# Cross-attention on one core: gram in nine matmuls per group, packed diagonal blocks, TensorE's orders rewritten

## What is computed

```python
probs_t = jax.nn.softmax(scores_t, axis=-1)
text_out = jnp.einsum('bhst,bhtd->bhsd', probs_t, v_t)
...
qsem = _l2norm(jnp.einsum('bhst,bte->bhse', probs_t, text_ehs))
sem = jnp.einsum('bhse,bne->bhsn', qsem, _l2norm(ip_ehs))
fused = attn_scores + SEM_SCALE * sem
probs_ip = jax.nn.softmax(fused, axis=-1) * spatial_mask[None, None, :, None]
...
out = (text_out + ip_out) @ W_out + b_out + residual
```

## Time and profile before

| | us |
|---|---|
| median of 3 runs | 386.72 |
| lowest and highest | 385.99, 387.68 |
| span of the profiled execution | 384.5 |
| busy in it: PE | 374.8 |
| DVE | 225.0 |
| ACT | 213.2 |
| POOL | 208.1 |

### The profile page before, as it was taken

The page is one execution under the profiler, slowest core; times in us unless marked ns, Lnnn a source line. Parts: engine busy times, 40 slices in busy tenths (PEclk is TensorE's granted clock), DMA queues, the critical chain, the costliest instruction groups (busy, mean ns, idle before and its releaser), DMA issues.

```text
span 384.5 us, 9489 instructions
## 1 busy us (share of the span) xinstructions
PE 374.8 (97%) x3610; PEld 320.3 (83%) x3610; DVE 225.0 (59%) x498; ACT 213.2 (55%) x498; POOL 208.1 (54%) x229
## 2 busy tenths in 40 slices
PE   8999999998999999999999999999999999999996
PEld 6879898777888888888888888888888888888774
DVE  4998462774457536664556646664556656654454
ACT  6834145575556554646556554646555476458742
POOL 7020470675448652796248642796258443855972
PEclk9999999999999999999999999999999999999999
DMA  8999998276027420571227430581207310001000
GB/s 252 321 241 182 201 213 157 82 162 140 9 72 166 78 72 2 157 147 24 76 73 162 81 87 2 160 147 20 77 2 174 59 43 3 2 2 57 2 3 31
DMA packets 30001, 37.88 MB, mean 99 GB/s; under 512 B 14378, under 2 KB 27163, under 8 KB 29275
## 3 DMA queue, kind: packets, MB, share of 16 engines
...
## 4 chain that ended last, share of the span: by engine, by line
PE 84%; DMA 6%; DVE 5%; ACT 2%; issue 1%; SPq 1%; DVEq 0%; ACTq 0%
PE PR L1078 39%; PE Y L1078 27%; PE O L1078 9%; PE P L1078 7%; DMA qst<-ma 3%; DVE mx L950 2%; DMA Vt<-wk 2%; PE PR L1269 1%; DMA qd<-kst 1%; PE PR L1206 1%; DVE kst L904 0%; DVE kst L902 0%; ACT big L796 0%; SPq L507 0%; SPq L427 0%
## 5 line engine op out<-in xcount | busy, mean ns | idle before, releaser
L620 POOL TENSOR_TENSOR pb<-pb 128x448 f32<-128x448 f32 x78 | 89.1, 1143 | 97.2 <-DVE pb L974 91.8
L950 DVE TENSOR_REDUCE mx<-PR 112x1 f32<-112x371 f32 x160 | 82.0, 537 | 75.2 <-PE PR L1078 74.9
L1078 PE MATMUL Y<-er,Gh 128*128 128x448 f32 x240 | 95.2, 397 | 0.7 <-ACT er L800 0.3
L974 DVE TENSOR_TENSOR pb<-big,Y 128x448 f32<-128x448 f32 x120 | 72.7, 620 | 33.6 <-PE Y L1078 33.4
L1078 PE MATMUL Y<-er,Gl 128*128 128x448 f32 x240 | 87.2, 363 | 0.0
L796 ACT ACTIVATE big<-P 128x448 f32<-128x448 f32 x120 | 65.2, 544 | 31.6 <-PE P L1078 31.4
L800 ACT ACTIVATE er<-big 128x448 fp32r<-128x448 f32 x120 | 69.3, 578 | 3.8
L1078 PEld LDWEIGHTS Y<-er,Gh 128*128 128x128 f32 x240 | 45.1, 188 | 11.9 <-DVE pb L974 7.8
L1078 PE MATMUL PR<-kst,qst 96*112 96x371 bf16 x160 | 50.6, 329 | 0.5 <-ACT Vt L788 0.2
L1078 PEld LDWEIGHTS Y<-er,Gl 128*128 128x128 f32 x240 | 45.2, 188 | 2.2
L1078 PE MATMUL P<-qst,kst 99*128 99x112 bf16 x480 | 43.0, 213 | 1.6 <-DMA qst<-ma 1.5
...
## 6 DMA issues: line engine op xcount, KB each, us to landing
...
```

The source lines that it names most:

```text
L620: pool.tensor_tensor(total, total, (pz, pm)[j], ALU.add).then_inc(s_S, 1)
L950: dve.tensor_reduce(mx[b % 2][:, h:h + 1], bank[0:S, 0:T], AX.X, ALU.max).then_inc(s_free[seq[u] % NR], 1)
L974: dve.tensor_tensor((pz, pm, pa[g % 2])[j], eb[g % 3][:, 448 * j:448 * j + 448], Y[y % 2][:, 0:448], ALU.mult).then_inc(s_P, 1)
L1078: return pe.matmul(o, st, mv, start=start, stop=stop, **kw)
```

## The change

**Packed diagonal blocks.** In e^T G e only the symmetric part of a diagonal block counts. So one matrix can hold both parts of it: its upper triangle with half the diagonal is the high part of G, its strictly lower triangle the low part. The matmul with `Gl` on the three diagonal blocks goes, 12 matmuls per group become 9 (5, 3 and 1 for j = 2, 1, 0), and off-diagonal blocks are no longer stored doubled; the total enters `O` with a factor 2 instead. The low part's diagonal must be zero for this. A new step takes half of it, `lh`, from every row and every column of `Gl`, and puts back what that removes through a 23rd value column (MV = 23) and two more operations on `R` (function `norms`).

**New units.** `D` and `L` run once per batch. `D`: DVE forms `dl` (half the diagonal of `Gl`, 128 x 384) and sums it to `lh`; POOL multiplies the diagonal blocks of `Gh` by a triangular mask. `L`: PE multiplies `dl` by ones (one matmul of 384 columns), ACT writes `lh` into the value column, DVE subtracts both from `Gl` in three operations, POOL masks the diagonal blocks of `Gl` and adds them to those of `Gh`. The first gram of a batch waits for that addition (`s_wd`).

**Orders.** All tables are rewritten. `g` is spelled out so that `g0` no longer follows `g1` at once, `E` stands behind `pT`, and `S2` before `v`.

```diff
-ROUNDS = ("S0 K0 m g m K1 S1 m v S2 m G0 m",
...
-          "S0 m g2 T0 T1 g1 g0 m r0 S1 m pw v S2 m V0 m",
-          "Kr S0 r1 m g m V1 m S1 m m v r2 mT S2 z GV",
-          "p E g2 g1 pT g0 S0 cT S1 v o S2")
...
+ROUNDS = ("K0 S0 m g2 m g1 S1 m K1 m S2 m g0 v G0",
...
+          "S0 m g2 T0 T1 g1 m g0 r0 S1 m pw S2 m v V0 m",
+          "Kr r1 m g2 g1 S0 m m g0 V1 S1 m m S2 v r2 mT z GV",
+          "p g2 pT E g1 D cT S0 S1 v g0 L o S2")
...
+                if u[0] == "D":
+                    b = u[1]
...
+                    for piece in g_pieces(b):
+                        freed(pool, seq[piece])
+                    diag = Gh[b % 2][:, :, 0:128]
+                    pool.tensor_tensor(diag, diag.bitcast(f32), tri[:, 0, :].unsqueeze(1).broadcast_to([128, 3, 128]),
+                                       ALU.mult).then_inc(s_wu, 1)
+                if u[0] == "L":
+                    b = u[1]
+                    diag, low = Gh[b % 2][:, :, 0:128], Gl[b % 2][:, :, 0:128]
+                    freed(pool, seq[u])
+                    pool.tensor_tensor(low, low.bitcast(f32), tri[:, 1, :].unsqueeze(1).broadcast_to([128, 3, 128]),
+                                       ALU.mult).then_inc(s_wu, 1)
+                    pool.wait_ge(s_wu, 2 * b + 2)
+                    pool.tensor_tensor(diag, diag.bitcast(f32), low.bitcast(f32), ALU.add).then_inc(s_wd, 1)
...
+            def norms(hs, square):
+                if square:
+                    dve.tensor_tensor(t1[:, hs], R[:, hs, 20], R[:, hs, 20], ALU.mult)
+                link(dve.tensor_tensor(lq[:, hs], R[:, hs, 20], R[:, hs, 22], ALU.mult))
+                link(dve.tensor_tensor(lq[:, hs], lq[:, hs], R[:, hs, 21], ALU.add))
+                dve.scalar_tensor_tensor(ssq[:, hs], t1[:, hs], EPS * EPS, lq[:, hs], ALU.mult, ALU.max).then_inc(s_clamp, 1)
...
+                    dve.scalar_tensor_tensor(dl[:, :, :], Gl[b % 2][:, :, 0:128].bitcast(f32), 0.5,
+                                             ident[:, :].unsqueeze(1).broadcast_to([128, 3, 128]),
+                                             ALU.mult, ALU.mult).then_inc(s_dl, 1)
...
+                        low = dve.scalar_tensor_tensor(gl, gl.bitcast(f32), lh[0:r, i:i + 1], bank[0:r, 128 * i:T],
+                                                       ALU.subtract, ALU.subtract)
...
                     if j == 2 and r == 0:
-                        freed(pe, seq[last_g(b)])
+                        pe.wait_ge(s_wd, b + 1)
...
-                    for i in range(j + 1):
-                        o = GOFF[i] + 128 * (j - i)
+                    for i in range(j):
+                        sl = slice(128 * (j - i), 128 * (j - i) + 128)
                         mv = er[g % 2][:, 448 * i:448 * i + 448]
-                        mm(d, Gh[b % 2][:, o:o + 128], mv, i == 0, False)
-                        last = mm(d, Gl[b % 2][:, o:o + 128], mv, False, i == j)
-                    last.then_inc(s_gram, 1)
+                        mm(d, Gh[b % 2][:, i, sl], mv, i == 0, False)
+                        mm(d, Gl[b % 2][:, i, sl], mv, False, False)
+                    mm(d, Gh[b % 2][:, j, 0:128], er[g % 2][:, 448 * j:448 * j + 448], j == 0, True).then_inc(s_gram, 1)
```

More of the change, by code:

```diff
@@ L87, in master_schedule @@
     order += [("G", 0, 0)] + split(1)[:2] + [("G", 0, 1)] + split(1)[2:] + [("G", 0, 2)] + [("K", 1, c) for c in range(3)] + [("Kr", 1)]
-    side = [("V", 0, 1), ("V", 0, 2)] + [("qip", b) for b in range(B)]
+    order += [("D", 0)]
+    side = [("V", 0, 1), ("L", 0), ("V", 0, 2)] + [("qip", b) for b in range(B)]
     side = [("V", 0, 0)] + spread(side[:-1], [("max", 0, h) for h in range(H)]) + side[-1:]
@@ L147, in behind @@
         else:
+            if u[0] == "D":
+                out, held = out + held, []
             out.append(u)
@@ L213, in build @@
         wol = sb("wol", [128, 3, C], f32r)
-        Gh = [sb(f"Gh{i}", [128, 768], f32r) for i in range(2)]
-        Gl = [sb(f"Gl{i}", [128, 768], f32r) for i in range(2)]
+        Gh = [sb(f"Gh{i}", [128, 3, TP], f32r) for i in range(2)]
+        Gl = [sb(f"Gl{i}", [128, 3, TP], f32r) for i in range(2)]
+        dl = sb("dl", [128, 3, 128], f32r)
+        lh = sb("lh", [128, 3])
+        ones_r = sb("ones_r", [128, 128], f32r)
+        tri = sb("tri", [128, 2, 128])
+        lq = sb("lq", [S, H])
         Vt = [sb(f"Vt{i}", [128, 3, H, MV]) for i in range(2)]
@@ L766, in _ @@
                                    ACT.Copy).then_inc(s_gh, 1)
+                elif k == "L":
+                    b = u[1]
+                    act.wait_ge(s_dl, 2 * b + 2)
+                    if b < 2:
+                        act.wait_ge(s_set, FILLS)
+                    else:
+                        act.wait_ge(s_pv, NG * (b - 1))
+                    act.activation(Vt[b % 2][:, :, :, 22], lh[:, :].unsqueeze(2).broadcast_to([128, 3, H]),
+                                   ACT.Copy, scale=2.0).then_inc(s_lc, 1)
                 elif k == "C":
@@ L777, in _ @@
                         act.wait_ge(s_pv, NG * (b - 1))
[L778 removed]
+                    act.activation(Gh[b % 2][0:r, 2, 0:a], bank[0:r, C:C + a], ACT.Copy)
                     act.activation(Vt[b % 2][0:r, 2, :, 16:20],
```

109 lines of the change are left out of this document (66 added, 43 removed), and 16 rows, old and new, of tables (EARLY, LAST, ROUNDS).

## The result

The changed kernel takes 388.64 us in the median of 16 runs, the kernel before 386.61 beside it; the ratio is 1.0062, 95% interval 1.0040 to 1.0085. So it is slower by 0.6%, where 384.1 and "faster" were forecast; the time lies within the range of 369 to 390. (A ratio here is not the quotient of two medians and can differ from it by up to 0.3%.) The mechanisms that the prediction named in the middle batches are there and cost less than forecast; the loss is before batch 0, at the end of batch 0, and in gains that batch 5 and the last batch did not bring.

What follows compares the result with a forecast made beforehand. PE, busy for 97% of 384.5 us, was taken as the bound. The terms +0.8, -2.7, +3.2, +2.0, -0.9, -1.8, -3.2 give -2.6: span 381.9, plus 2.2 around it, 384.1 us; range 380 to 387, 8 in 10 within 369 to 390.

Steps and rivals of the forecast that it cites:

- Before batch 0, +0.8: Before the first gram: D and L put 2.2 us of DVE work ahead of the maxima; all but 0.8 us hidden.
- The end of batch 0: Boundary behind batch 0: POOL's mask steps make the next first gram 3.2 us later; the scores' DMA lands as before.
- Middle batches, PE's work: Batches 1 to 4: PE's work alone becomes 3.5 us shorter per batch, 39.6 us.
- First wait: Batch ends: first gram waits for POOL's third mask step, 2.6 us behind batches 1 to 4, 1.2 and 0.3 behind 5, 6.
- Second wait: Third round: three chained DVE operations wait for POOL's additions, so PE waits 1.4 us at a maximum, six times.
- rival (a): Third round: the chained DVE operations slip in and cost nothing; 375.7 to 378.7 us, say 377; chance 0.20.
- Rival (b): Batch boundaries: POOL is in time; 14.6 us less, about 369.5, or about 361 without the other wait too; chance 0.15.
- Batch 5, -0.9: Batch 5: -3.5 us of PE work, +1.4 for the DVE chain, +1.2 for POOL's masks: 0.9 us shorter.
- Batch 6, -1.8: Batch 6: -3.5 us of PE work, +1.4 for the DVE chain, +0.3 for POOL's masks: 1.8 us shorter.
- The last batch, -3.2: Last batch: five groups save 0.6 us each and some 0.6 of waits, 0.4 given back: 3.2 us shorter.
- Rival (c), the clock: Batch boundaries: PE's clock falls to half while it waits, 1.8 us at each of seven boundaries; 396.7 us; chance 0.10.

Runs made afterwards that it cites:

- e2: Changed kernel with only the loads of `tri` and `ident` issued some 20 us earlier, right behind wv's: 386.82 us.
- e4: Kernel before (twelve matmuls, no mask steps) with all order tables of the changed kernel: 384.74 us.
- e10: Kernel before with only the changed kernel's order tables for the middle batches and the first rounds of batches 1 and 6: 382.23 us.
- e6: e2 with POOL's three mask steps per batch left out, so diagonal blocks go in unmasked: 378.95 us.
- e11: e2 with the second and third mask step moved from POOL to DVE, nothing left out: 380.42 us.
- e7: e2 without the two DVE operations that join the halves of the squared norms: 384.39 us.
- e8: e2 with S0 moved behind cT, and v ahead of S2, in round 4 of batches 5 and 6: 383.97 us.
- e3: Changed kernel with the order tables of the kernel before, D and L put into them, prologue as changed: 391.16 us.
- e15: e2 with the edits of e8 and e11, filler matmuls ahead of two transfer waits, and T0, T1 earlier in the last batch's first round: 377.15 us.
- e9: e2 with unit E behind unit L in round 4 of batches 1 to 4, and K0 and K1 later: 398.48 us.

## Why the prediction was wrong, by its own steps

The forecast was 384.1 us, 2.6 less than before; it came out 2.0 more. By stretches its steps miss by +5.5 before the first gram, +4.0 in batch 0, -5.1 in the four middle batches, +1.5 in batch 5, +0.1 in batch 6 and +3.0 in the last: +9.0 of span in the profiled execution, whose span is some 4 us above that of the median runs. The medians miss by 4.5 us.

- **Before batch 0, +0.8: its result was right and a DMA was left out.** "The idle time there hides all but 0.8" counted the instructions of D and L, and e2 bears out the 0.8 (67.8 against 67.0), though they take 3.0 us on DVE there (1.24, 0.55, 1.21) and not 2.2. It did not count the load of `tri` that D waits for, 2.36 us, nor that PE behind it could drop to the lower clock, here for 10.2 us. In the medians the load costs 1.8 us (e2), not the 5.5 of this trace.
- **The end of batch 0: the step that failed is "the scores wait there for a DMA that lands 6.3 us after mT in either order".** It landed after 10.9. The new orders and the gains of that stretch brought mT1 forward by 3 us, the keys' load stayed, and the rows landed when the load let them, 12.2 to 14.3 us behind its order. e4, with twelve matmuls, has 3.9 of the 4.9 us of e2's pause, and e10, with the old tables there, has 0.3. The mask steps, which the prediction made the limit there, cost PE 0.7 us behind so long a pause.
- **Middle batches, PE's work: mis-sized.** 39.6 us were forecast, 40.20 came. The orders gave 0.8 (0.6 forecast); 15 matmuls less and one more gave 2.0 (42.20 to 40.20) in place of 2.8. I took the pace inside a run of matmuls, 0.20 us, for each of the 15. Why a removed one was worth less is not settled.
- **First wait: right in place and cause, 2.6 forecast, 1.2 to 1.6 measured.** POOL's third step ended 10.44 us behind `pT` (10.6 forecast), PE stood ready at 8.76 (8.05 forecast). e6 removes the wait with its cause, and e11 removes most of it without leaving anything out. Behind batches 5 and 6 the waits were 0.0 and 0.5 (1.2 and 0.3 forecast). Here the prediction's view was of most use: the repair comes straight from it.
- **Second wait: the step that failed is "the second behind the second addition".** 1.4 us were forecast, six times; e7 gives 0.2. Lines 900 and 901 both ran round the end of the first addition, only line 902 waited for the second one (1.03 us) and ended 4.98 us behind T0, before PE's maximum at 5.09. So rival (a) was the truer case here; I had weighed it at 0.20 because row L1039 of the earlier trace rows waited, yet the earlier trace rows also had L1017 slip in. (Rival (b) writes "without the first wait too" where its 8.4 us are this second wait.)
- **Batch 5, -0.9: the new `LATE` was not looked at.** It brings S0 ahead of `g0`, where it waits for mT6's transfers, 2.1 us in the changed kernel and 2.7 in e2. e8 undoes that and yields 39.3 us, 1.7 less than before.
- **Batch 6, -1.8: 1.7 measured, by luck.** PE's work there fell by 2.5 us (37.96 to 35.45) and not by 3.5, and the waits added 0.8 us and not 1.7: the two misses cancel.
- **The last batch, -3.2: five groups' matmuls were counted as time, though PE does not bound it.** The row of before for it was there to be read:

```profile
349.90:384.50 34.60, 29.82 (x343) 23.76 (x339) 17.75 (x47) 17.87 (x44) 21.49 (x26) 0.98 0.08 22
```

PE idles for 4.8 us in it. With nine matmuls it idles for 6.4, and the time stays. With no maxima to fill in, PE waits for the exponentials (1.37 us, also in e4) and at the end for the image tokens' chain, where the joined norms cost 0.75 (e7). Order and matmuls do not add up here: twelve matmuls in the old order take 34.6 us, in the new 35.2 (e4), nine in the old 36.5 (e3), in the new 34.5. What sets the length is not shown: e15 was to move the chain forward and moved it back. That stays open.
- **Rival (c), the clock: true as a mechanism, and here at other places.** At the middle boundaries of the changed kernel waits of 1.2 to 1.6 us left the clock at 1.00; where e9 made them 2.0 us it fell behind three of four. In the changed kernel it fell at four other places, in or behind pauses of 1.3 (before batch 0), 6.7, 2.1 and 1.4 us. "TensorE: Matmul & The Clock Gate" of the Trainium skill, section "Part 1: The HAM clock gate", has idleness bring the clock to half; the trace agrees there.

That the time came within the range is luck: misses of both signs met, 5.1 us gained in the middle against 14 lost elsewhere.
